# First attention: windowed softmax read from the own block of the full scores, shifts by block as extra contraction rows, a correction for the full softmax

## The chip, the cores and the metric

The kernel runs on one core of one Trainium2 chip. The metric is the device time of one execution in microseconds, the median of the runs shown. TensorE is called PE, VectorE DVE, ScalarE ACT, GpSimd POOL, and SyncE, which only issues DMAs here, SP.

## What is computed

Four layers on x of shape 8 x 512 x 128, float32: a first attention, a routed SwiGLU layer, a causal attention, a second expert layer. Only the first attention is touched. It has 16 heads of 8 columns and adds three softmaxes over the same q, k and v, cut here to what matters:

```python
qkv = x @ w_qkv                       # x is layer-normalised; 8 sequences of 512 tokens
s_loc = einsum("bnihd,bnjhd->bnhij", qw, kw) * scale   # 4 windows of 128 tokens
s_dil = einsum("bighd,bjghd->bghij", qd, kd) * scale   # tokens of equal index mod 4
s_glb = einsum("bihd,bjhd->bhij", q, k) * scale        # all 512 tokens
o = (softmax(s_loc) @ vw + softmax(s_dil) @ vd + softmax(s_glb) @ v) / 3
x = x + o @ w_out
```

## The kernel before, in words

`attention` is written once and called twice; `causal` is False for the first attention. Each sequence is a batch b of 8, and its 16 heads are four groups g of 4 heads. A slot n = 4b + g is one group of one sequence; there are 32. Queries and keys are split into three bfloat16 parts each, so one contraction over 72 of 96 partitions gives float32-like scores: `QS` and `KS`, one 512-column row per head, with the partitions above holding small extra rows.

Per slot the stages are these, each a function of the same name on every engine that takes part in it:

- `smax`: 16 matmuls (4 heads x 4 query blocks) of queries against all 512 keys into one of two PSUM banks `SM`; DVE reduces each to 16 maxima per query (4 windows x 4 phases) in `M`. PE may be two ahead of DVE.
- `maxima` (DVE): from `M` the row maxima of the three softmaxes, split in three bfloat16 parts (`maxima_parts`, `MT`); `rows`: PE transposes them, DVE copies them to `MR`, SP sends them to `QS` and `ML` by six DMAs.
- `scores`: twelve units into two halves of `ST`. Units 0 to 3 are mixed: one head's windowed scores in one bank and its dilated ones in the other, each by a matmul of 3 rows that subtracts the maxima (L422) and four of 128 columns (L430). Units 4 to 11 are full: two matmuls of 512 columns (L434), the shift among the contraction rows. ACT takes the exponential of each unit, 1024 columns, into a ring `E` of eight.
- `pv`: three rounds into `OA`, four heads side by side on 32 output columns each. Round 0 does the windowed and the dilated values (L457, 16 matmuls each), rounds 1 and 2 the full ones (L463). The matmuls are float32, so each counts as two in the trace.
- `evac` (ACT) copies `OA` out; `sel` (PE L472) turns it by query and picks outputs and sums; DVE divides and adds the three softmaxes (L679 to L690).

Projections (`proj`, `part1`, `left1`, `part2`, `left2`, `parts_out`, `stacks`), `values`, `heads_T` and `out_proj` come once a batch and are spread over its four slots.

The order is written out by hand in `slot(n)`: `put(i, name, which)` places an event behind unit i of slot n, and every engine walks the same list and takes the events it has a part in. Slot n carries the row maxima of slot n + 1 (the late ones, up to unit `CUT` - 1) and of n + 2 (the early ones). `maxima` of n + 1 stands behind unit `CUT` - 1, `rows` behind `CUT` + 1. Each engine runs its own list strictly in order. `MI` is one PSUM bank that `rows`, `sel`, `values` and the batch events take turns in.

## Time and profile before

| | |
|---|---|
| median of 3 runs | 2044.01 us |
| lowest and highest | 2037.59 and 2047.19 us |
| the profiled execution | 2029.46 us |
| its span | 2027.8 us |
| its mean granted TensorE clock | 0.898 |
| PE, DVE, ACT, POOL busy | 80%, 57%, 44%, 30% of the span |

The first attention fills 74 to 824 us of the span; ahead of it lie loads, the first projection and the first stacks. Rows of the trace name an instruction by its line, its engine and output <- input, with the tiles' names; the first attention's begin with w, the second's with c. A duration of a matmul holds its drain, so the time from one start to the next is what one costs in a row of them. An idle time stands with what ended it. The granted clock is 1 at 2.4 GHz and 0.5 at 1.2 GHz.

### The profile page before, as it was taken

The page shows a single profiled execution, that of the slowest core. Times are in us where ns is not written, and L with a number is a line of the kernel's source. Part 1 is how long each engine was busy: PE and PEld are TensorE (multiplying, and loading weights), DVE is VectorE, ACT ScalarE, POOL GpSimd, SP SyncE. Part 2 cuts the span into 40 slices and gives each one's busy share as a digit, 9 for nine tenths or more (in the row PEclk, how much of TensorE's full clock was granted, in tenths as well). Part 3 has the DMA queues.
Part 4 walks back from the last instruction along what each step waited for, and adds up shares of the span by engine and source line. Part 5 has one row for each costly group of instructions (what it writes and reads, how often), then busy time and mean ns, then how long its engine had stood idle before and what let it go on. Part 6 is the DMA issues. An engine that isn't in the chain of part 4 may idle for free. (4 is left out here: it accounts for less than half of the span.)

```text
span 2027.8 us, 35597 instructions
## 1 busy us (share of the span) xinstructions
PE 1630.1 (80%) x11387; PEld 888.1 (44%) x11489; DVE 1157.7 (57%) x3354; ACT 883.5 (44%) x1406; POOL 616.0 (30%) x879
## 2 busy tenths in 40 slices
PE   1899999999999999579899994468888888616683
PEld 1244444444444443355566663124444444514563
DVE  4756676656667664226333333468888877344584
ACT  1255555656565655431133331045555555402242
POOL 1001010101010100003522223376666533454467
PEclk8699999999999999679999997589999999557897
DMA  3110101111111100322011111233333220235442
GB/s 104 37 52 23 45 22 46 28 42 35 42 39 29 42 26 3 125 42 43 9 40 43 43 43 27 61 69 75 75 75 74 68 64 27 82 121 148 128 115 58
DMA packets 92786, 115.08 MB, mean 57 GB/s; under 512 B 13977, under 2 KB 76223, under 8 KB 92350
## 3 DMA queue, kind: packets, MB, share of 16 engines
q1 hardware_dynamic: 75710, 91.10, 16.5%
q0 software_dynamic: 16896, 21.69, 4.6%
q8 instruction: 99, 1.62, 0.3%
q14 instruction: 81, 0.66, 0.1%
HBM read 73.93 MB, written 39.34 MB: 56 GB/s over the span
## 5 line engine op out<-in xcount | busy, mean ns | idle before, releaser
L543 ACT ACTIVATE we<-wst 128x1024 f32<-128x1024 f32 x384 | 386.1, 1025 | 303.4 <-PE wst L430 158.8
L625 DVE TENSOR_REDUCE wm<-wsm 128x16 f32<-128x512 f32 x512 | 335.7, 685 | 259.5 <-PE wsm L393 255.6
L622 DVE CUSTOM_DVE_ANT_0 cjunk<-csm,const 128x128 bf16<-128x128 f32 (+3 forms) x512 | 232.5, 486 | 78.9 <-PE csm L393 70.3
L543 ACT ACTIVATE ce<-cst 128x896 f32<-128x896 f32 (+1 forms) x256 | 179.2, 704 | 186.0 <-PE cst L417 184.6
L393 PE MATMUL wsm<-wks,wqs 96*128 96x512 bf16 x512 | 191.3, 398 | 32.8 <-DMA wks<-qk_parts 20.2
L393 PE MATMUL csm<-cks,cqs 96*128 96x128 bf16 (+3 forms) x512 | 157.8, 315 | 69.1 <-DVE cnm L622 43.1
L772 POOL TENSOR_SCALAR_AFFINE_SELECT ce<-ce 128x256 f32<-128x256 f32 x256 | 125.3, 506 | 160.0 <-ACT ce L543 159.2
L434 PE MATMUL wst<-wqs,wks 128*128 128x512 bf16 x442 | 139.2, 385 | 9.5 <-issue 5.3
L1606 DVE TENSOR_TENSOR abhh<-absg,abup 128x512 f32<-128x512 f32 x72 | 49.5, 688 | 152.5 <-ACT absg L1585 152.5
L463 PE MATMUL woa<-we,wv 128*32 128x512 f32 x1024 | 132.0, 636 | 1.6 <-ACT we L543 1.6
L393 PEld LDWEIGHTS csm<-cks,cqs 96*128 96x128 bf16 x512 | 51.1, 100 | 182.6 <-DVE cnm L622 117.3
L1622 POOL DMA_INDIRECT abxb<-rows,asource x72 | 68.2, 947 | 162.3 <-DVE abys L1613 145.6
L417 PE MATMUL cst<-cqs,cks 128*128 128x384 bf16 (+3 forms) x480 | 106.6, 299 | 5.0 <-ACT ce L543 1.3
L422 PE MATMUL wst<-wml,const_b 3*128 3x512 bf16 x256 | 100.1, 391 | 9.3 <-ACT we L543 9.3
L430 PE MATMUL wst<-wqs,wks 96*128 96x128 bf16 x1024 | 105.9, 227 | 0.0
L1585 ACT ACTIVATE absg<-abup 128x512 f32<-128x512 f32 x72 | 43.0, 597 | 140.4 <-PE abup L1554 140.4
L393 PEld LDWEIGHTS wsm<-wks,wqs 96*128 96x128 bf16 x512 | 47.6, 98 | 122.5 <-DVE wm L625 61.0
L463 PE MATMUL coa<-ce,cv 128*32 128x512 f32 (+3 forms) x1024 | 92.3, 482 | 8.5 <-POOL ce L772 8.5
L430 PEld LDWEIGHTS wst<-wqs,wks 96*128 96x128 bf16 x1024 | 63.0, 108 | 60.1 <-issue 60.1
L761 POOL COPY wv<-wvs 128x128 f32<-128x128 f32 x32 | 9.3, 290 | 228.4 <-ACT wvs L503 200.2
L1554 PE MATMUL abup<-awg,abxt 128*128 x144 | 75.1, 604 | 2.3 <-ACT abxt L1591 2.3
L1574 PE MATMUL aby<-awd,abht 128*128 x576 | 76.2, 276 | 0.1
(318 smaller groups left out, 2987.7 us busy)
## 6 DMA issues: line engine op xcount, KB each, us to landing
wqs<-qk_parts SPq DMA_DIRECT2D x96, 96.0 KB
wks<-qk_parts SPq DMA_DIRECT2D x96, 96.0 KB
cqs<-qk_parts SPq DMA_DIRECT2D x96, 96.0 KB
cks<-qk_parts SPq DMA_DIRECT2D x96, 96.0 KB
b1r<-rows SPq DMA_DIRECT2D x40, 194.0 KB, 2.6
qk_parts<-wpt SPq DMA_DIRECT2D x48, 128.0 KB, 2.4
qk_parts<-cpt SPq DMA_DIRECT2D x48, 128.0 KB, 2.4
b0r<-rows SPq DMA_DIRECT2D x40, 130.0 KB, 2.5
```

The costliest lines, as they stand in the source:

```text
L393: pe.matmul(SM[:, j % 2, 0:keys], QS[0:MR0, h, t * P:(t + 1) * P], KS[0:MR0, h, 0:keys], start=True, stop=True, skip_group_check=True).the ...
L417: m = pe.matmul(st[:, at:at + width], KS[:, h, kb * P:(kb + 1) * P], QS[:, h, kb * P:S], start=True, stop=True, skip_group_check=True)
L422: pe.matmul(st[:, at:at + S], const["ones_b"][0:SPLIT, :], ML[:, g % 2, kind * HG + hs, :], start=True, stop=False, skip_group_check=True)
L430: m = pe.matmul(out, k, q, start=False, stop=(t == NT - 1), skip_group_check=True)
L434: m = pe.matmul(st[:, c * S:(c + 1) * S], KS[:, h, kb * P:(kb + 1) * P], QS[:, h, :], start=True, stop=True)
L463: m = pe.matmul(OA[VW * hs:VW * (hs + 1), S - width:S], V[:, kb, g * HG + hs, 0:VW], E[:, e_slot(g, HG * r + hs), at:at + width], start=(c ...
L543: act.activation(E[:, e_slot(g, i), 0:width], ST[:, (U * g + i) % 2, 0:width], ACT.Exp, scale=SCALE).then_inc(s_ex, 1)
L622: dve.tensor_tensor_reduce(JUNK[:, j % 4, 0:keys], SM[:, j % 2, 0:keys], const["mask_wide"][:, S - keys:S], 1.0, -3e38, ALU.add, ALU.max, ...
L625: dve.tensor_reduce(M[:, hs, t, :].rearrange("p (w f) -> p w f", f=DIL), SM[:, j % 2, :].rearrange("p (w i f) -> p w f i", w=NT, f=DIL), A ...
L772: pool.affine_select(e, e, [[0, 2], [1, P]], ALU.is_ge, 0.0, base=0, channel_multiplier=-1).then_inc(s_tri, 1)
L1554: m = pe.matmul(UP[:, i % 2, w, 0:F], XT[:, i % 2, :], weight[:, bass.ds(e * F, F)], start=True, stop=True)
L1574: m = pe.matmul(Y[:, j % 2, 0:D], HT[:, j % 2, c * P:(c + 1) * P], WD[:, bass.ds(e * HB * D + c * D, D)], start=(c == 0), stop=(c == HB - 1))
```

## The change

For the first attention only:

- The windowed softmax gets no scores of its own. Its scores are the own block of the full scores. Each block of keys kb has its own shift per query: the local maximum where kb is the query's own window, the maximum over the row elsewhere. So `QS` gets twelve rows of shifts (4 blocks x 3 bfloat16 parts) and three for the dilated shift; `KS` gets one-hot rows (`marks`) that pick the block's.
- There are ten units a slot: 0 to 7 are full (L437), 8 and 9 are dilated, two heads each (a shift matmul of 15 rows on partitions 96 to 110, L442, and four of 128 columns, L445).
- `pv` rounds 0 and 1 take each block's own quarter to the windowed columns of `V` and the rest to the full ones (ten pieces in place of four, L469); round 2 is the dilated one (L476).
- The full softmax's sum and output lack the own block in its scale, so a factor `E1`, the exponential of the difference of both maxima, joins them in `sel`.
- DVE's `maxima` has four more operations, one for each block's shifts (L688), and a difference (L692), and its parts are 80 columns wide instead of 48. ACT computes `E1` and copies `MR` (L585). POOL adds the three softmaxes. SP sends one DMA of rows per slot in place of six, and in the causal attention one in place of three.
- `CUT` is 3 instead of 4, and events move in `slot(n)`: `sel` from behind unit 4 to behind unit 5, the batch events likewise.

```diff
     L = "c" if causal else "w"
     KINDS = 1 if causal else 3
-    U = 8 if causal else 12
-    R = U // HG
+    SHIFTS = 1 if causal else NT + 1
+    U = 8 if causal else 10
+    R = 2 if causal else 3
     SMU = HG * NT
-    MROWS = KINDS * HG * SPLIT
-    CUT = 2 if causal else 4
+    MROWS = SHIFTS * HG * SPLIT
+    MR1 = MR0 + SHIFTS * SPLIT
+    CUT = 2 if causal else 3
     AHEAD = SMU * (U - CUT) // U
...
                 put(3, "evac", n - 1)
-                put(4, "sel", n - 1)
                 put(9, "pv", n, 1)
                 put(CUT - 1, "maxima", n + 1)
                 put(CUT + 1, "rows", n + 1)
+                put(5, "sel", n - 1)
...
-                elif i < HG:
-                    for kind in range(2):
-                        at = kind * S
-                        pe.matmul(st[:, at:at + S], const["ones_b"][0:SPLIT, :], ML[:, g % 2, kind * HG + hs, :],
-                                  start=True, stop=False, skip_group_check=True)
-                        for t in range(NT):
-                            q, k, out = QS[0:MR0, h, :], KS[0:MR0, h, :], st[:, at:at + S]
-                            if kind == 0:
-                                q, k, out = window(q, t), k[:, t * P:(t + 1) * P], window(out, t)
-                            else:
-                                q, k, out = q[:, t * P:(t + 1) * P], k[:, t::DIL], out[:, t * P:(t + 1) * P]
-                            m = pe.matmul(out, k, q, start=False, stop=(t == NT - 1), skip_group_check=True)
+                elif i < 2 * HG:
+                    for c in range(2):
+                        kb = 2 * (i // HG) + c
+                        m = pe.matmul(st[:, c * S:(c + 1) * S], KS[:, h, kb * P:(kb + 1) * P], QS[:, h, :],
+                                      start=True, stop=True)
                 else:
                     for c in range(2):
-                        kb = 2 * (i // HG - 1) + c
-                        m = pe.matmul(st[:, c * S:(c + 1) * S], KS[:, h, kb * P:(kb + 1) * P], QS[:, h, :],
-                                      start=True, stop=True)
+                        h, at = g * HG + 2 * (i - 2 * HG) + c, c * S
+                        pe.matmul(st[:, at:at + S], const["dil_b"][MR0:MR1, :], QS[MR0:MR1, h, :], start=True, stop=False,
+                                  skip_group_check=True)
+                        for t in range(NT):
+                            m = pe.matmul(st[:, at + t * P:at + (t + 1) * P], KS[0:MR0, h, t::DIL],
+                                          QS[0:MR0, h, t * P:(t + 1) * P], start=False, stop=(t == NT - 1),
+                                          skip_group_check=True)
                 m.then_inc(s_st, 1)
...
-                pe.wait_ge(s_tri if causal else s_ex, U * n + HG * (r + 1))
+                pe.wait_ge(s_tri if causal else s_ex, U * n + min(HG * (r + 1), U))
...
+                elif r < 2:
+                    for c in range(2):
+                        kb = 2 * r + c
+                        pieces = [(kb, kb + 1, 2 * VC)] + [(a, z, 0) for a, z in ((0, kb), (kb + 1, NT)) if a < z]
+                        for a, z, col in pieces:
+                            for hs in range(HG):
+                                e = E[:, e_slot(g, HG * r + hs), c * S:(c + 1) * S]
+                                m = pe.matmul(span(OA[VW * hs:VW * (hs + 1), :], a, z),
+                                              V[:, kb, g * HG + hs, col:col + VW], span(e, a, z),
+                                              start=(kb == 0 and a == 0), stop=False, skip_group_check=True)
+                else:
+                    for t in range(NT):
+                        for hs in range(HG):
+                            at = (hs % 2) * S + t * P
+                            m = pe.matmul(OA[VW * hs:VW * (hs + 1), t * P:(t + 1) * P], VP[:, t, g * HG + hs, :],
+                                          E[:, e_slot(g, 2 * HG + hs // 2), at:at + P], start=False, stop=(t == NT - 1),
+                                          skip_group_check=True)
                 m.then_inc(s_pv, 1)
...
+            def maxima(n, g, b, turn):
+                if causal:
+                    return
+                act.wait_ge(s_dif, n + 1)
+                if n >= NG:
+                    act.wait_ge(s_no, NNO * (n - NG + 1))
+                act.activation(E1[:, g, :], DIF[:, g, :], ACT.Exp, scale=SCALE).then_inc(s_e1, 1)
+
+            def rows(n, g, b, turn):
+                if causal:
+                    return
+                act.wait_ge(s_full, turn + 1)
+                if n:
+                    act.wait_ge(s_ml, 16 * n)
+                act.activation(MR[:, :], MI[0:MROWS, 0:S // 2].bitcast(BF16), ACT.Copy).then_inc(s_mr, 1)
...
-                dve.tensor_reduce(NM[:, 2 * HG:3 * HG, :], own, AX.X, ALU.max, negate=True).then_inc(s_mp, 1)
-                dve.wait_ge(s_mp, 4 * n + 3)
-                dve.tensor_reduce(NM[:, HG:2 * HG, :].rearrange("p h t -> p (h t)"),
+                dve.tensor_reduce(NM[:, NT * HG:(NT + 1) * HG, :], own, AX.X, ALU.max, negate=True).then_inc(s_mp, 1)
+                dve.wait_ge(s_mp, 8 * n + 3)
+                dve.tensor_reduce(LOC[:, :, :].rearrange("p h t -> p (h t)"),
                                   MD[:, :, :, :].rearrange("p h t k -> p (h t) k"), AX.X, ALU.max, negate=True
                                   ).then_inc(s_mp, 1)
-                dve.wait_ge(s_mp, 4 * n + 4)
+                dve.wait_ge(s_mp, 8 * n + 4)
+                for w_ in range(NT):
+                    dve.scalar_tensor_tensor(NM[:, w_ * HG:(w_ + 1) * HG, :], LOC[:, :, :], const["own"][:, w_:w_ + 1],
+                                             GLB[:, :, :], ALU.min, ALU.max).then_inc(s_mp, 1)
+                if n >= NG:
+                    dve.wait_ge(s_e1, n - NG + 1)
+                dve.tensor_tensor(DIF[:, g, :].rearrange("p (h t) -> p h t", h=HG), GLB[:, :, :], LOC[:, :, :], ALU.subtract
+                                  ).then_inc(s_dif, 1)
+                dve.wait_ge(s_mp, 8 * n + 8)
                 maxima_parts(n)
...
+                e1 = E1[:, g, :].rearrange("p (h t) -> p t h", h=HG)
+                dve.wait_ge(s_e1, n + 1)
+                dve.tensor_tensor(T1[:, :, :], e1, got[:, :, 0:HG, DH], ALU.mult).then_inc(s_no, 1)
+                dve.reciprocal(RL[:, :, 0:2 * HG, :], got[:, :, 0:2 * HG, DH:OC]).then_inc(s_no, 1)
                 dve.wait_ge(s_no, NNO * n + 1)
-                if b:
-                    dve.wait_ge(s_ot, b)
-                out = ON[:, :, g * HG * DH:(g + 1) * HG * DH]
-                to = out.rearrange("p t (h c) -> p t h c", h=HG) if causal else PR[:, :, :, :]
-                dve.tensor_tensor(to, got[:, :, :, 0:DH], RL[:, :, :, :].broadcast_to([P, NT, k, DH]), ALU.mult
+                dve.tensor_tensor(DEN[:, :, :], T1[:, :, :], got[:, :, 2 * HG:3 * HG, DH], ALU.add).then_inc(s_no, 1)
+                dve.wait_ge(s_no, NNO * n + 3)
+                dve.reciprocal(RL[:, :, 2 * HG:3 * HG, 0], DEN[:, :, :]).then_inc(s_no, 1)
+                dve.wait_ge(s_no, NNO * n + 4)
+                dve.tensor_tensor(T1[:, :, :], e1, RL[:, :, 2 * HG:3 * HG, 0], ALU.mult).then_inc(s_no, 1)
+                dve.wait_ge(s_no, NNO * n + 5)
+                dve.tensor_tensor(RL[:, :, 0:HG, 0], RL[:, :, 0:HG, 0], T1[:, :, :], ALU.add).then_inc(s_no, 1)
+                dve.wait_ge(s_no, NNO * n + 6)
+                if n:
+                    dve.wait_ge(s_on, 2 * n)
+                dve.tensor_tensor(PR[:, :, :, :], got[:, :, :, 0:DH], RL[:, :, :, :].broadcast_to([P, NT, k, DH]), ALU.mult
                                   ).then_inc(s_no, 1)
-                if causal:
-                    return
-                dve.wait_ge(s_no, NNO * n + 2)
-                dve.tensor_reduce(out, PR[:, :, :, :].rearrange("p t (k h) c -> p t (h c) k", k=KINDS), AX.X,
-                                  ALU.add).then_inc(s_no, 1)
...
-                dve.memset(KS[64:P, :, :], -1.0 if causal else 1.0).then_inc(s_ones, 1)
+                dve.memset(KS[64:P if causal else MR0, :, :], -1.0 if causal else 0.0).then_inc(s_ones, 1)
...
+            def sel(n, g, b, turn):
+                if causal:
+                    return
+                pool.wait_ge(s_no, NNO * (n + 1))
+                if b:
+                    pool.wait_ge(s_ot, b)
+                out = ON[:, :, g * HG * DH:(g + 1) * HG * DH].rearrange("p t (h c) -> p t h c", h=HG)
+                pool.tensor_tensor(out, PR[:, :, 0:HG, :], PR[:, :, HG:2 * HG, :], ALU.add).then_inc(s_on, 1)
+                pool.wait_ge(s_on, 2 * n + 1)
+                pool.tensor_tensor(out, out, PR[:, :, 2 * HG:3 * HG, :], ALU.add).then_inc(s_on, 1)
...
-                if n >= 2:
-                    sp.wait_ge(s_st, U * (n - 1))
-                for i in range(SPLIT):
-                    k = KINDS * HG * i
-                    sp.dma_start(QS[MR0 + i:MR0 + i + 1, g * HG:(g + 1) * HG, :],
-                                 MR[k:k + HG, :]).then_inc(s_ml, 16)
-                    if not causal:
-                        sp.dma_start(ML[i:i + 1, g % 2, :, :],
-                                     MR[k + HG:k + 3 * HG, :]).then_inc(s_ml, 16)
+                if n >= NG:
+                    sp.wait_ge(s_st, U * (n - NG + 1))
+                sp.dma_start(QS[MR0:MR1, g * HG:(g + 1) * HG, :], MR[:, :]).then_inc(s_ml, 16)
...
+    marks = np.zeros((P, NT), np.float32)
+    dil = np.zeros(P, np.float32)
+    for i in range(SPLIT):
+        at = MR0 + i * (NT + 1)
+        marks[at:at + NT] = np.eye(NT)
+        dil[at + NT] = 1.0
```

Two places show how the order moved. The first is PE's list from the last two row maxima of slot n + 1 (the `wsm` x2 that end them) to `rows`. L393 and L408 are row maxima, L434 and L437 full scores, L472 `sel`, L457 windowed and dilated PV, L400 and L415 `rows`. Before, behind the last two row maxima:

```order
L434 MATMUL wst<-wqs,wks 128x512 [waits wex]
L434 MATMUL wst<-wqs,wks 128x512
L393 MATMUL wsm<-wks,wqs 128x512 [waits wmx,wrd1]
L472 MATMUL wmi<-const,wos 128x108 [waits wev,wvs]
L472 MATMUL wmi<-const,wos 128x108 x3
L434 MATMUL wst<-wqs,wks 128x512 [waits wex]
L434 MATMUL wst<-wqs,wks 128x512
L393 MATMUL wsm<-wks,wqs 128x512 [waits wmx]
L457 MATMUL woa<-we,wv 32x4x32 [waits wev,wvc,wex]
L457 MATMUL woa<-we,wv 32x4x32 x15
L457 MATMUL woa<-we,wvp 32x128 x16
L400 MATMUL wmi<-const_b,wmt 36x128 [waits wms,wno]
```

And in the changed kernel, with those last two as the first row of row maxima:

```order
L408 MATMUL wsm<-wks,wqs 128x512 [waits wmx] x2
L437 MATMUL wst<-wqs,wks 128x512 [waits wex]
L437 MATMUL wst<-wqs,wks 128x512
L408 MATMUL wsm<-wks,wqs 128x512 [waits wmx,wrd2]
L408 MATMUL wsm<-wks,wqs 128x512 [waits wmx]
L437 MATMUL wst<-wqs,wks 128x512 [waits wex]
L437 MATMUL wst<-wqs,wks 128x512
L408 MATMUL wsm<-wks,wqs 128x512 [waits wmx]
L415 MATMUL wmi<-const_b,wmt 60x128 [waits wms,wno]
L415 MATMUL wmi<-const_b,wmt 60x128 x3
L437 MATMUL wst<-wqs,wks 128x512 [waits wex]
L437 MATMUL wst<-wqs,wks 128x512
```

Before, the second row maximum of the next set is followed by 32 PV matmuls, and `sel` stands ahead of it. Now two come together behind one unit and a third behind the next, and two more row maxima, a PV round and `sel` follow the rows shown.

The second place is DVE's list behind the same point, from the first operation of `maxima` on. Before:

```order
L636 TENSOR_REDUCE wnm<-wm 128x16 [waits wms,wmx]
L639 TENSOR_TENSOR wmd<-wm,const 128x256
L645 TENSOR_REDUCE wnm<-wm 128x16
L647 TENSOR_REDUCE wnm<-wmd 128x16 [waits wmp]
L661 CAST wmt<-wnm 128x12x4 [waits wmr,wmp]
L665 TENSOR_TENSOR wnr<-wnm,wmt 128x48 [waits wms]
L661 CAST wmt<-wnr 128x12x4 [waits wms]
L665 TENSOR_TENSOR wmt<-wnr,wmt 128x12x4 [waits wms]
L625 TENSOR_REDUCE wm<-wsm 128x16 [waits wsm]
L679 RECIPROCAL wrl<-wmi 128x48 [waits wfull]
L685 TENSOR_TENSOR wpr<-wmi,wrl 128x384 [waits wot,wno]
L690 TENSOR_REDUCE won<-wpr 128x4x32 [waits wno]
```

And in the changed kernel:

```order
L672 TENSOR_REDUCE wglb<-wm 128x16 [waits wms,wmx]
L675 TENSOR_TENSOR wmd<-wm,const 128x256
L681 TENSOR_REDUCE wnm<-wm 128x16
L683 TENSOR_REDUCE wloc<-wmd 128x16 [waits wmp]
L688 SCALAR_TENSOR_TENSOR wnm<-wloc,const,wglb 128x16 [waits wmp]
L688 SCALAR_TENSOR_TENSOR wnm<-wloc,const,wglb 128x16 x3
L692 TENSOR_TENSOR wdif<-wglb,wloc 128x16 [waits we1]
L705 CAST wmt<-wnm 128x20x4 [waits wmr,wmp]
L709 TENSOR_TENSOR wnr<-wnm,wmt 128x80 [waits wms]
L705 CAST wmt<-wnr 128x20x4 [waits wms]
L709 TENSOR_TENSOR wmt<-wnr,wmt 128x20x4 [waits wms]
L661 TENSOR_REDUCE wm<-wsm 128x16 [waits wsm] x5
```

The group of maxima has grown from 8 operations to 13, and `sel`, which stood one row maximum behind it, is now five behind and, as the diff shows, has seven operations instead of three.

## Rows read from the trace of the kernel before

**Rows 1.** The page: the span.

```profile
span 2027.8 us, 35597 instructions
```

**Rows 2.** Stretch of the first attention: stretch, length, busy and count per engine, clock, DMA.

```profile
core 0: us, PE busy (x) PEld busy (x) DVE busy (x) ACT busy (x) POOL busy (x), PEclk, DMA share, GB/s
74.00:824.00 750.00, 699.43 (x5889) 320.81 (x5958) 463.93 (x951) 433.27 (x484) 56.35 (x102) 0.97 0.12 33
```

**Rows 3.** Groups by line, 74 to 824 us: busy, mean ns, idle before, what ended it.

```profile
L543 ACT ACTIVATE we<-wst 128x1024 f32<-128x1024 f32 x383 | 385.2, 1025 | 303.4 <-PE wst L430 158.8 <-PE wst L434 142.4
L625 DVE TENSOR_REDUCE wm<-wsm 128x16 f32<-128x512 f32 x488 | 320.2, 685 | 245.0 <-PE wsm L393 242.2
...
L383 PE MATMUL wmi<-w,wxnT 128*128 128x128 f32 x112 | 23.1, 349 | 0.0
...
L369 PE MATMUL wmi<-wxnT,w 128*128 128x512 f32 x28 | 14.8, 612 | 1.3 <-ACT wxnT L503 1.3
```

**Rows 4.** Timeline of PE in one slot: start us, us, instruction, count, idle before.

```profile
438.25 0.39 PE L422 MATMUL wst<-wml,const_b 3*128 3x512 bf16 x1
438.57 0.40 PE L430 MATMUL wst<-wqs,wks 96*128 96x128 bf16 x4
...
439.47 0.59 PE L393 MATMUL wsm<-wks,wqs 96*128 96x512 bf16 x2
...
441.33 1.11 PE L472 MATMUL wmi<-const,wos 128*128 128x108 f32 x8 [0.22 <-ACT wos L550]
442.28 0.59 PE L434 MATMUL wst<-wqs,wks 128*128 128x512 bf16 x2
442.71 0.38 PE L393 MATMUL wsm<-wks,wqs 96*128 96x512 bf16 x1
443.02 1.08 PE L457 MATMUL woa<-we,wv 128*32 128x128 f32 x32
443.92 1.06 PE L457 MATMUL woa<-we,wvp 128*32 128x128 f32 x32
...
449.68 1.93 PE L463 MATMUL woa<-we,wv 128*32 128x512 f32 x16
```

**Rows 5.** Timeline of PE: the first and the thirty-first `sel`.

```profile
109.25 1.11 PE L472 MATMUL wmi<-const,wos 128*128 128x108 f32 x8 [0.23 <-ACT wos L550]
...
812.08 2.01 PE L472 MATMUL wmi<-const,wos 128*128 128x108 f32 x8 [1.26 <-ACT wos L550]
```

**Rows 6.** Timeline of DVE in the same slot: maxima and `sel` groups.

```profile
441.21 0.42 DVE L636 TENSOR_REDUCE wnm<-wm 128x16 f32<-128x256 f32 x1
...
443.69 0.69 DVE L625 TENSOR_REDUCE wm<-wsm 128x16 f32<-128x512 f32 x1
444.29 0.45 DVE L679 RECIPROCAL wrl<-wmi 128x48 f32<-128x48 f32 x1
...
445.88 0.68 DVE L625 TENSOR_REDUCE wm<-wsm 128x16 f32<-128x512 f32 x1
```

**Rows 7.** Groups by line, whole span: small DVE operations of both attentions.

```profile
L679 DVE RECIPROCAL wrl<-wmi 128x48 f32<-128x48 f32 x32 | 14.4, 450 | 31.1 <-PE wmi L472 31.1
...
L679 DVE RECIPROCAL crl<-cmi 128x16 f32<-128x16 f32 x32 | 8.2, 256 | 15.3 <-PE cmi L472 14.5
...
L665 DVE TENSOR_TENSOR cnr<-cnm,cmt 128x16 f32<-128x16 f32 x32 | 6.2, 195 | 1.1
```

**Rows 8.** Timeline of DVE at the start: the fills of QS and KS.

```profile
24.85 3.47 DVE L699 MEMSET wqs<- 64x4096 uint32 x1 [0.91 <-issue]
...
29.98 6.88 DVE L700 MEMSET wks<- 64x8192 bf16 x1 [1.66 <-issue]
```

**Rows 9.** Clock: two stretches, then a PV round and four matmuls of the second layer.

```profile
826.00:950.00 124.00, 91.74 (x385) 59.41 (x380) 51.43 (x191) 42.08 (x94) 19.54 (x33) 0.75 0.39 86
406.00:414.00 8.00, 8.00 (x50) 3.14 (x50) 1.98 (x3) 2.64 (x3) 0.00 (x0) 0.79 0.42 114
...
408.37 3.54 PE L463 MATMUL woa<-we,wv 128*32 128x512 f32 x16
...
844.42 1.09 PE L1390 MATMUL atp<-const,arows 128*128 128x128 f32 x4 [5.21 <-ACT arows L1442]
...
857.60 0.66 PE L1390 MATMUL atp<-const,arows 128*128 128x128 f32 x4 [2.22 <-ACT arows L1442]
```

More of the change, by code:

```diff
@@ L865, in setup @@
     C = sb("const", [P, c_dram.shape[1]])
[L866 removed]
+    CB = sb("const_b", [P, 4 * P], BF16)
     W0 = sb("w0", [P, 3 * D])
@@ L873, in setup @@
     const["mask_wide"] = C[:, at["open"][0]:at["mask_q"][1]]
-    for i, name in enumerate(("ident", "ones", "before")):
+    for i, name in enumerate(("ident", "ones", "before", "dil")):
         const[name + "_b"] = CB[:, i * P:(i + 1) * P]
```

119 lines of the change are left out of this document (68 added, 51 removed).

## The prediction

> **What bounds the kernel now.** I read the page for the span [rows 1], then the stretches for the first attention, which runs from about 74 to 824 us [rows 2]: PE is busy 699.4 of 750 us there, VectorE (DVE) 463.9, ScalarE (ACT) 433.3. So the question is what sets PE's pace. The groups by line say how the others stand [rows 3]: ACT's exponentials take 1025 ns each and ACT idles for 303 us in front of them, waiting for PE; DVE's row maxima (the wm reduces) take 685 ns and DVE idles 245 us, again for PE. The reader should see that neither is a bound as long as PE always has something that it may issue. The `sel` matmuls come once a slot: the 1st and the 31st start at 109.25 and 812.08 us [rows 5], so a slot lasts 702.83/30 = 23.4 us, and 32 slots make the stage.
>
> The timeline of one slot [rows 4] gives PE's issue prices, start to start, since a duration contains about 0.16 us of drain. A unit of mixed scores (438.25 to 439.47) costs 1.22. A full unit (442.28 to 442.71) costs 0.43, say 0.44. A row-maximum matmul costs 0.59 for two less the drain, 0.22. `sel` (441.33 to 442.28) costs 0.95. The windowed local PV (443.02 to 443.92) costs 0.90, the dilated one as much, and a round of full PV 1.93 less a little drain, 1.86. DVE's rows [rows 6] give the two groups that hold up its queue: maxima and their parts run from 441.21 to 443.69, 2.48 us; reciprocal, product and sum of `sel` from 444.29 to 445.88, 1.59 us. PE hides the first under `sel` and 1.8 us of windowed PV, both placed right after it. That is the fact that the change touches.
>
> **The change, part by part.** PE, a slot: four mixed units become two dilated ones, 2 x 1.22 = 2.44 off. The windowed local PV goes, 0.90 off. The ten pieces of own and foreign blocks stream the same columns as the four full ones, and the windowed row shows that a 128-column piece costs a quarter of a 512-column one (0.90/4 = 0.22 against 1.86/4 = 0.47 per block for two rounds, that is 0.93 per 512 columns), so they add nothing. In all 3.34 us a slot, 107 us in 32 slots, if PE never waited longer.
>
> ACT: two exponentials less (2.05 us), the copy of rows (some 0.6) and a tiny exponential more. It idles anyway: nothing, as long as it isn't held. The tiny exponential does hold it: it waits for DVE's difference, and behind it stand the exponential of unit 3, `evac` and the copy of rows. The difference is there some 1.9 us into DVE's group, and 1.9 + 0.25 + 1.02 = 3.2 is less than the wait of PE below. Nothing added.
>
> DVE: the maxima group gains four small operations, a difference, and parts of 80 instead of 48 columns. The nearest rows [rows 7] are 195 ns for a dependent 128x16 operation; independent ones overlap, so I take 0.09 to 0.15 for each of these five (0.6) and 0.17 for the longer parts: 2.48 + 0.77 = 3.25 us. Bounds: 2.48 (all hidden in each other's drain) and 3.9 (all five at full price and more on the parts). `sel` loses the final sum (to POOL) and 16 reciprocals but gets four dependent small operations and a reciprocal of 16 columns (256 ns against 450 ns for 48): 1.59 - 0.51 - 0.1 + 4 x 0.2 + 0.26 = 2.05 us. Bounds 1.6 and 2.4. The copy of rows (0.35) leaves DVE.
>
> Now the order, which the two places in the section on the change show. DVE does maxima after unit 2, then five row maxima, then `sel`. PE behind the 16th row-maximum matmul has two scores units and two such matmuls it may issue (there are two SM banks), then a third that needs DVE to be through the whole group. I count from the start of the 16th: 0.85 until DVE is done with the 15th, 0.65 for the 16th, 3.25 for the group, 0.65 for the next reduce, 0.19 back: **5.6 us**, in which PE has 0.22 + 2 x 0.44 + 2 x 0.22 = 1.5 us of work. It waits 4.1 us. `sel` and windowed PV, which covered this group before, now come later. Then PE works 4.3 us (row maximum, rows, a unit, two row maxima, PV, `sel`), and DVE's `sel` group holds the next row maxima: 0.2 + 2.05 + 0.65 + 0.19 = 3.1 us, with 1.3 of work in it. The rest of the loop is PE's: two dilated units, a full PV, three full units, the dilated PV, seven row maxima, 8.6 us with 0.35 of waiting. Sum 5.6 + 4.3 + 3.1 + 8.6 = 21.6 us, and the projections, values and so on, once a batch, 37.9/28 = 1.35 a slot from the two larger groups [rows 3]: **23.0 us**. The slot of now is 23.4, of which the clock (0.97 granted, [rows 2]) is 3%, 22 us over the stage, some of it at the start: 22.9 without. So the 107 us of PE's work turn into waits: +0.1 a slot, +3 us.
>
> Start: the fill of KS goes from 6.88 us to the form that took 3.47 [rows 8], ahead of the first stacks: -3 us. The four `marks` lie under the first stacks' transfers. POOL's two sums a slot and the one transfer of rows in place of six (three to one in the second attention) have 8 us before anyone needs them: nothing; if that cover went, it would be 1 us or less a slot.
>
> **The clock.** The rows show its price and its cause [rows 9]. In the stretch 406 to 414 the granted clock was 0.79, and the full PV in it took 3.54 us instead of 1.93: 1.6 us a drop. From 826 to 950, where PE was busy 91.7 of 124 us, in pieces, 0.75 was granted; after an idle time of 5.21 us four matmuls took 1.09 us (1.2 GHz), after one of 2.22 us the same four took 0.66 (2.4 GHz). A wait of 4.1 us lies between these. I take it that it costs one drop a slot, 0.8 of it on work: 1.3 x 32 = +42 us; half of the stage's present drops, which come in runs of mixed units, go: -7.
> The Trainium skill (TensorE: Matmul & The Clock Gate, "Why this matters for your kernels") asks for no long idle gaps of PE between bursts, or the clock falls to half rate. By that rule the new wait brings the drop in every slot, which is the forecast; the 5.21 us row agrees, and no row here shows a gap of just 4 us.
>
> Sum: +3 - 3 + 42 - 7 = **+35 us**. The profiled execution took 2029.5 us (span 2027.8), 14.6 below the median of 2044.0 and below the lowest of the three runs; I add the difference to the median: **2079 us**, own range 2058 to 2100.
>
> **Rivals.**
> A second drop a slot, at the 1.8 us wait for `sel`: another 42 us, 2120. For it: PE is then busy about 17 of 24 us, near the 74% of 826 to 950 us. Against: the 2.22 us row.
> No drop at all: 2044 + 3 - 3 = 2044. For it: the gap of 2.22 us cost none. Against: 4.1 lies nearer to the 5.21.
> DVE's groups at their lower bounds, 2.48 and 1.6: both waits shrink, 1.2 us a slot, 39 us; the long wait is then 3.3 us and the clock may hold: 2044 - 39 = 2005. This decides from a maxima group of some 2.6 us down. Against: the added operations depend on each other and can't all vanish.
> The shift matmul overlaps its neighbours. Its 15 rows lie on partitions 96 up, those of the four that follow on 0 to 95, while now both use the lowest ones. Then its 0.30 us (438.25 to 438.57 is the start of the next group, [rows 4]) is hidden, four times a slot: 38 us off, 2041 with the drops and 2003 without.
> The Trainium skill (TensorE: Matmul & The Clock Gate, "Part 3: Packing small matmuls") says that matmuls on different row groups run at the same time; by it this case would hold in full. Nothing in the trace runs on disjoint partitions, so no row bears it out; here both add into the same bank.
>
> **How the numbers follow.** Forecast 0.44, second drop 0.15, both slower; no drop 0.12; short DVE groups 0.15; overlap 0.14 (0.04 of it ends near no change). A measurement here can tell 0.5%, 10 us, from no change. Faster 0.25, same 0.16, slower 0.59. The range 2005 to 2125 leaves out the ends of the overlap and the worst of the drops.
>
> **What would show it.** PE's row maxima (wsm) waiting on DVE some 4 us once and 2 us once a slot; a maxima group of 3.25 us; PE's busy time in the stage down by about 100 us with the stage no shorter; many short stretches of granted clock 0.5, a mean of about 0.9. Wrong, if that wait is under 2 us, if the clock stays at 0.97, or if a dilated unit takes under 1.0 us.

## The result, and the profile after

| | median | lowest, highest | profiled span | its clock | first attention, 72 us to its last `heads_T` | clock there |
|---|---|---|---|---|---|---|
| before | 2040.8 us | 2036.4, 2047.2 | 2027.8 us | 0.898 | 760 us | 0.97 |
| changed | 2161.9 us | 2156.4, 2163.3 | 2154.7 us | 0.838 | 884 us | 0.81 |

The changed kernel is slower: the ratio is 1.0586 (1.0548 to 1.0623), 121 us by the medians. The sign was forecast, the size was not: 2162 us lies beyond the 2125 at the top of the range. The spans differ by 126.9 us and the first attention by 124; the rest took 1199 us after and 1196 before. So all but some 3 us of it is in the stage that the prediction looked at.

The page of the changed kernel, its span, busy times and clock, which answer to [rows 1]. What to see is the row PEclk: from its second digit on, where the first attention is, it stands at 6 to 8.

```profile
span 2154.7 us, 35568 instructions
...
PE 1654.8 (77%) x11361; PEld 908.6 (42%) x11361; DVE 1179.4 (55%) x3611; ACT 851.5 (40%) x1410; POOL 643.9 (30%) x943
...
PEclk8678788787878788876899999767999999757997
```

The stage as one stretch (columns as in [rows 2]), of the kernel before and then of the changed one:

```profile
72.00:832.00 760.00, 704.98 (x5918) 322.98 (x5988) 467.33 (x957) 435.67 (x486) 56.35 (x102) 0.97 0.12 33
```

```profile
72.00:956.00 884.00, 718.50 (x5855) 340.89 (x5853) 489.13 (x1205) 395.72 (x484) 84.50 (x166) 0.81 0.10 28
```

PE is busy longer with less work, because the same work takes twice the time at half the clock. With the busy time at the low clock (303 us, before 46) counted half it is 567 us, before 682: 115 less. Length times granted clock takes that out: it is what the stage would last at 2.4 GHz, and the rest is lost to the clock. Before, 760 x 0.97 = 737 and 23 lost; after, 884 x 0.81 = 716 and 168 lost. **The schedule got 21 us shorter and the clock took 145 us.** (Waiting at the low clock loses nothing and is counted here. It is little: I went through the stage in stretches of 1 us, and those below 0.75 are 324 us long with PE busy in 303 of them. The printed clocks have two digits. With the clock of every 1 us stretch added up, 25 us were lost before and 164 after: 15 us by the schedule and 139 by the clock. So the two terms are good to some 6 us.)

The waits of PE in the stage of the changed kernel (line, releaser, us in total, times, longest), then the group of the row maxima. Of before's matmul L393 the same view has 6.2 us in 28 times.

```profile
PE wsm L408 <- DVE wm L661: 140.8, 85, 4.1
PE wmi L362 <- DVE wpr L750: 7.3, 6, 1.2
PE wmi L415 <- DVE wmt L709: 3.7, 1, 3.7
```

```profile
L661 DVE TENSOR_REDUCE wm<-wsm 128x16 f32<-128x512 f32 x487 | 313.4, 684 | 258.0 <-PE wsm L408 256.3
```

The timeline of PE in one slot of the changed kernel, which answers to [rows 4]:

```profile
499.72 0.38 PE L408 MATMUL wsm<-wks,wqs 96*128 96x512 bf16 x1
...
501.49 0.60 PE L437 MATMUL wst<-wqs,wks 128*128 128x512 bf16 x2
505.41 0.39 PE L408 MATMUL wsm<-wks,wqs 96*128 96x512 bf16 x1 [3.33 <-DVE wm L661]
505.73 0.41 PE L415 MATMUL wmi<-const_b,wmt 128*60 128x128 bf16 x4
...
507.39 3.22 PE L469 MATMUL woa<-we,wv 128*32 128x128 f32 x40
510.54 1.14 PE L485 MATMUL wmi<-const,wos 128*128 128x108 f32 x8
...
512.60 0.38 PE L408 MATMUL wsm<-wks,wqs 96*128 96x512 bf16 x1
514.15 0.39 PE L408 MATMUL wsm<-wks,wqs 96*128 96x512 bf16 x1 [1.17 <-DVE wm L661]
514.47 0.38 PE L442 MATMUL wst<-wqs,const_b 15*128 15x512 bf16 x1
514.79 0.41 PE L445 MATMUL wst<-wqs,wks 96*128 96x128 bf16 x4
515.13 0.39 PE L442 MATMUL wst<-wqs,const_b 15*128 15x512 bf16 x1
```

And DVE's in the same slot, which answers to [rows 6]:

```profile
501.24 0.42 DVE L672 TENSOR_REDUCE wglb<-wm 128x16 f32<-128x256 f32 x1
...
502.66 0.67 DVE L688 SCALAR_TENSOR_TENSOR wnm<-wloc,const,wglb 128x16 f32<-128x16 f32 x4
503.24 0.17 DVE L692 TENSOR_TENSOR wdif<-wglb,wloc 128x16 f32<-128x16 f32 x1
...
504.46 0.52 DVE L709 TENSOR_TENSOR wmt<-wnr,wmt 128x80 bf16<-128x80 f32 x1
504.67 1.88 DVE L661 TENSOR_REDUCE wm<-wsm 128x16 f32<-128x512 f32 x3
...
511.72 0.18 DVE L737 TENSOR_TENSOR wt<-we,wmi 128x16 f32<-128x16 f32 x1 [3.36 <-PE wmi L485]
...
512.51 0.18 DVE L744 TENSOR_TENSOR wt<-we,wrl 128x16 f32<-128x16 f32 x1
512.73 0.17 DVE L746 TENSOR_TENSOR wrl<-wrl,wt 128x16 f32<-128x16 f32 x1
512.94 0.56 DVE L750 TENSOR_TENSOR wpr<-wmi,wrl 128x384 f32<-128x384 f32 x1
513.41 0.68 DVE L661 TENSOR_REDUCE wm<-wsm 128x16 f32<-128x512 f32 x1
```

The reader should see three things. The maxima group takes 504.67 - 501.24 = 3.43 us, and behind it the third row-maximum matmul starts 505.41 - 499.72 = 5.7 us after the 16th. The `sel` group takes 513.41 - 511.72 = 1.69 us and makes PE wait a second time. And the PV round behind the first wait took 3.22 us, where the same 40 matmuls take 1.94 at full clock.

Why the PV round took longer is seen in the stretches of this slot (columns as in [rows 2]):

```profile
486.00:497.00 11.00, 11.00 (x71) 4.82 (x71) 2.01 (x4) 2.89 (x4) 1.00 (x4) 0.53 0.12 40
501.00:507.00 6.00, 2.54 (x13) 0.87 (x12) 5.34 (x17) 3.35 (x6) 0.00 (x0) 0.97 0.00 0
507.00:510.00 3.00, 3.00 (x38) 1.63 (x40) 1.29 (x2) 0.74 (x1) 0.00 (x0) 0.50 0.09 26
510.00:517.00 7.00, 5.78 (x44) 2.93 (x36) 5.11 (x20) 2.96 (x3) 2.18 (x4) 0.99 0.00 0
517.00:524.00 7.00, 7.00 (x52) 2.95 (x53) 2.48 (x8) 1.54 (x2) 0.00 (x0) 0.52 0.27 67
```

In this slot the waits themselves lie at 2.4 GHz, and the clock falls to 1.2 GHz when PE is already at work again: once 1.6 us behind the end of the 3.3 us wait, and once 2.9 us behind the end of the 1.2 us wait. In the low stretches PE is busy throughout. In other slots the clock has already fallen when the long wait ends, as in this one, whose single row maximum takes 0.61 us instead of 0.39:

```profile
167.22 0.61 PE L408 MATMUL wsm<-wks,wqs 96*128 96x512 bf16 x1 [3.32 <-DVE wm L661]
```

In the stage after there are 56 low stretches and the start of one more, 324 us in all. That is 1.75 a slot of 5.8 us each, 3 to 11 us apiece. Of the 32 waits over 2.5 us, 22 have one beginning within 2 us of their end, mostly of 3 or 4 us; of the 29 waits of 1.2 us, 23 have one beginning 1 to 3 us behind them, mostly of 6 to 11 us. Some ten have no wait over 1 us near.

In the stage before I count 10, 48 us in all. The first, 15 us, is the stage's start, where the clock stands at 0.50 from 60 to 72 us already:

```profile
72.00:87.00 15.00, 14.59 (x54) 5.34 (x55) 9.64 (x26) 4.91 (x5) 1.80 (x4) 0.50 0.15 41
```

The other nine all begin at the end of a slot's mixed units or right behind it, eight of them with no wait of PE over 0.5 us in the 8 us ahead.

The prediction's sum lacked one thing beside the clock. Of those 32 waits over 2.5 us seven last 4.1 us. In just these seven slots the last operation of DVE's maxima group takes 1.3 us, and a POOL operation of the q and k preparation (L808) runs beside it; in the other 24 rows of that operation in the stage it takes 0.5 and POOL has nothing running. From the timelines of POOL and of DVE:

```profile
559.03 1.15 POOL L808 TENSOR_TENSOR wqr<-wqk,wpt 128x512 f32<-128x512 f32 x1 [3.44 <-ACT wpt L538]
```

```profile
559.24 1.32 DVE L709 TENSOR_TENSOR wmt<-wnr,wmt 128x80 bf16<-128x80 f32 x1
```

Why it takes longer there isn't shown; no run moves the POOL operation.

### The profile page after: what moved, and what is told of

It reads as the page before. It is cut to its first block and busy times, and to the rows that moved or that the text cites. A ratio compares the mean times of both kernels' runs of the same rounds, so it can differ in the third digit from the quotient of the medians.

```text
span 2154.7 us, 35568 instructions
## 1 busy us (share of the span) xinstructions
PE 1654.8 (77%) x11361; PEld 908.6 (42%) x11361; DVE 1179.4 (55%) x3611; ACT 851.5 (40%) x1410; POOL 643.9 (30%) x943
## 5 line engine op out<-in xcount | busy, mean ns | idle before, releaser
L556 ACT ACTIVATE we<-wst 128x1024 f32<-128x1024 f32 x320 | 322.6, 1021 | 343.1 <-PE wst L437 268.7
L408 PE MATMUL wsm<-wks,wqs 96*128 96x512 bf16 x512 | 212.5, 461 | 165.7 <-DVE wm L661 143.2
L408 PE MATMUL csm<-cks,cqs 96*128 96x128 bf16 (+3 forms) x512 | 160.7, 322 | 65.6 <-DVE cnm L658 39.7
L833 POOL TENSOR_TENSOR won<-wpr 128x128 f32<-128x128 f32 x32 | 14.5, 453 | 657.4 <-DVE wpr L750 657.4
L469 PE MATMUL woa<-we,wv 128*32 128x128 f32 (+2 forms) x2560 | 187.3, 461 | 0.0
L408 PEld LDWEIGHTS wsm<-wks,wqs 96*128 96x128 bf16 x512 | 55.2, 111 | 284.6 <-DVE wm L661 212.2
L437 PE MATMUL wst<-wqs,wks 128*128 128x512 bf16 x512 | 170.4, 419 | 1.1 <-ACT we L556 1.0
L469 PEld LDWEIGHTS woa<-we,wv 128*32 128x32 f32 x2560 | 97.3, 148 | 86.7 <-issue 80.2
L408 PEld LDWEIGHTS csm<-cks,cqs 96*128 96x128 bf16 x512 | 51.6, 101 | 181.0 <-DVE cnm L658 109.6
L432 PE MATMUL cst<-cqs,cks 128*128 128x512 bf16 (+3 forms) x512 | 115.6, 309 | 1.9 <-ACT ce L556 1.3
L1628 PE MATMUL abup<-awu,abxt 128*128 x144 | 74.4, 598 | 0.0
L437 PEld LDWEIGHTS wst<-wqs,wks 128*128 128x128 bf16 x512 | 44.8, 102 | 69.4 <-issue 43.4
```

What stands on the lines that cost most here:

```text
L408: pe.matmul(SM[:, j % 2, 0:keys], QS[0:MR0, h, t * P:(t + 1) * P], KS[0:MR0, h, 0:keys], start=True, stop=True, skip_group_check=True).the ...
L432: m = pe.matmul(st[:, at:at + width], KS[:, h, kb * P:(kb + 1) * P], QS[:, h, kb * P:S], start=True, stop=True, skip_group_check=True)
L437: m = pe.matmul(st[:, c * S:(c + 1) * S], KS[:, h, kb * P:(kb + 1) * P], QS[:, h, :], start=True, stop=True)
L469: m = pe.matmul(span(OA[VW * hs:VW * (hs + 1), :], a, z), V[:, kb, g * HG + hs, col:col + VW], span(e, a, z), start=(kb == 0 and a == 0), ...
L556: act.activation(E[:, e_slot(g, i), 0:width], ST[:, (U * g + i) % 2, 0:width], ACT.Exp, scale=SCALE).then_inc(s_ex, 1)
L1628: m = pe.matmul(UP[:, i % 2, w, 0:F], XT[:, i % 2, :], weight[:, bass.ds(e * F, F)], start=True, stop=True)
```

## The experiments

All ratios are to the kernel before, run on the same chip beside each (its medians were 2035.6 for the first four, 2044.3 for the next four, 2038.8 for the last two). "Lost" is length x (1 - clock) of the stage from 72 us to its end, the rest "at full clock". Gains and losses in us against the changed kernel are differences of medians taken beside other medians of the kernel before; by the ratios they come out up to 9 us otherwise (96 instead of 105 us for the cover). The main theory, A in the expectations, is that the waits cost little as time and much by the clock. Its rivals put the loss on the longer DVE groups as plain waiting (B), on new matmuls dearer than reckoned (C), on one long group as such (D), or on ACT being held (E). A1 and A2 ask whether the short wait or the short matmuls of the dilated units start the drops that remain.

### Fill the long wait with useless matmuls

```diff
+                if not causal and j == 2 and n >= 2 and FILL:
+                    pe.wait_ge(*emptied(turn))
+                    for _ in range(FILL):
+                        pe.matmul(MI[:, :], QS[0:MR0, h, t * P:(t + 1) * P], KS[0:MR0, h, :], start=True, stop=True, skip_group_check=True)
```

The changed kernel with `FILL` = 16, then 8. The results of these matmuls are never read.

> The changed kernel with 16 extra matmuls of 512 columns a slot, into the idle MI bank, ahead of the third early row maximum, where PE waits about 4 us for DVE. Their results are overwritten. They are 16 x 0.22 = 3.5 us of work that nobody needs. Theory A (the waits themselves cost nothing more than the 107 us saved; what made the kernel slower is that the granted clock falls in and after each wait, some 10 us of each slot's 28 at 1.2 GHz): with PE kept going the drop that follows this wait mostly goes, while the one at the wait for sel may stay; the mean clock in the stage rises from 0.82 to 0.88 or more and the kernel is 50 to 90 us faster than the changed one, 2070 to 2110 us. Theory B (the hand-over between PE and DVE sets the pace and the clock only mirrors it): no gain, 2160 us or some 5 us more. Theory C (the new matmuls, PV in ten pieces and shifts by 15 rows, are dearer than reckoned): no gain either, 2160 to 2270 us, as the extra work adds 3.5 us a slot where it is not hidden.

> The changed kernel with 8 extra matmuls in place of e1_fill16's 16, 1.7 us of work in the wait of some 4 us. Theory A (the loss is the granted clock): PE is kept going for part of the wait, so part of the gain comes, between the changed kernel's 2162 and the 2074 of the run with 16: about 2115 us, stage clock 0.86. Theory B (the fuller queue helped in some other way): the same 2074 us or the 2162 us of no filling, not in between.

Sixteen: 2073.8 us, 1.0163 (1.0122 to 1.0204). **The kernel does some 3.5 us more on PE in a slot and is 88 us faster.** The timeline of PE in a slot of it:

```profile
518.29 3.62 PE L409 MATMUL wmi<-wks,wqs 96*128 96x512 bf16 x16
522.59 0.39 PE L414 MATMUL wsm<-wks,wqs 96*128 96x512 bf16 x1 [0.68 <-DVE wm L667]
...
524.22 1.94 PE L475 MATMUL woa<-we,wv 128*32 128x128 f32 x40
...
529.70 0.39 PE L414 MATMUL wsm<-wks,wqs 96*128 96x512 bf16 x1 [1.17 <-DVE wm L667]
```

The filler stands where the wait was, and the PV round is back at 1.94 us. This is one of the seven slots with the wait of 4.1 us: from the last full unit before the filler to the row maximum behind it are 4.73 us, 4.74 in such a slot of the changed kernel, so the row maximum starts no later. The 1.17 us wait is as before: 18 of 30 such waits still have a low stretch close behind, and 24 low stretches of 138 us are left in the stage:

```profile
72.00:882.00 810.00, 741.47 (x6333) 364.33 (x6331) 487.91 (x1204) 394.10 (x484) 84.48 (x166) 0.92 0.11 31
```

Lost to the clock: 65 us instead of 168. At full clock the stage is 745 us, 29 more than in the changed kernel. This is as theory A has it; B and C had no gain.

Eight: 2138.1 us, 1.0467 (1.0403 to 1.0531), 24 us better than none. I had expected about 2115, half of what sixteen bring; it is a quarter. It lies between none and sixteen, where the rival named for this run had no place. The stage shows 862 us at 0.85, 129 lost. The clock does not answer in proportion to the wait.

### Bring the cover back

```diff
-            put(2 if causal else 1, "pv", n - 1, R - 1)
+            put(2 if causal else 3, "pv", n - 1, R - 1)
-                put(5, "sel", n - 1)
+                put(4, "sel", n - 1)
```

The changed kernel with the dilated PV behind unit 3 and `sel` behind unit 4, so that PE has them to do while DVE is in its maxima group.

> The changed kernel with two events moved: the dilated PV of the slot before from behind unit 1 to behind unit 3, and sel from behind unit 5 to behind unit 4. Nothing is added or left out. PE then has 0.9 us of PV in the wait for the maxima group, and DVE meets the work of sel before it has fallen behind. Theory A: both waits shrink by 0.9 us together and with them the drops: a slot of 25 instead of 28 us, 2060 to 2090 us. Theory B: the slot shortens by the 0.9 us of wait alone, 28 to 30 us over 32 slots, 2130 us. Theory C: 2130 to 2160 us.

2057.3 us, 1.0116 (1.008 to 1.0152): 105 us back, 3 us beyond what A expected at best, and far from B and C. PE's waits for `wm` fall from 140.8 to 63.5 us; 688 us at full clock, 103 lost.

### Cut the group as well

```diff
+                put(3, "max_b", n + 1)
+                put(4, "max_c", n + 1)
+                put(5, "max_e", n + 1)
+                put(5, "rows", n + 1)
-                put(CUT + 1, "rows", n + 1)
...
-                    put(9, "out_proj", b - 1)
...
+                    put(6, "out_proj", b - 1)
...
```

The edit above, and DVE's `maxima` cut in three behind units 2, 3 and 4, so that row maxima come in between; the small exponential and `rows` behind unit 5; `out_proj` a slot later. No operation is added or removed.

> As e2_cover, and the maxima group of DVE is cut in three: the three operations that read the row maxima behind unit 2, local maxima, shifts and difference behind unit 3, the three bfloat16 parts behind unit 4, with row-maximum reduces between them; rows go behind unit 5, the small exponential behind unit 5, and the output projection to the next slot. The same operations, in another order. PE then never waits over 1.5 us for a row maximum. Theory A: the clock stays at 0.95 or more in the stage and the 3.3 us of PE's work that the change removed come through: a slot of 20.5 to 21.5 us against 23.4 before, 1960 to 1990 us, faster than both kernels. Theory B: a slot of 23 us or so, about 2040. Theory C: 2100 us or more.

**1943.4 us, 0.9537 (0.9499 to 0.9575): 4.6% below the kernel before and 10% below the changed one.** It is also some 17 us below what I had expected at best. The stage, then PE's waits in it:

```profile
72.00:750.00 678.00, 612.11 (x5853) 308.42 (x5852) 481.29 (x1204) 393.75 (x484) 84.83 (x166) 0.95 0.13 37
```

```profile
PE wsm L411 <- DMA wks<-qk_parts: 21.3, 7, 4.6
PE wmi L418 <- DVE wpr L761: 20.0, 27, 1.0
PE wsm L411 <- DVE wm L664: 5.7, 19, 1.9
```

At full clock 644 us, 93 less than before: now most of the 107 us of PE's work that the change removes comes through (some 4 of the 93 are the earlier start). 34 us are lost to the clock. What is late next is the first stacks of a batch (21.3 us in 7 times). In a slot, DVE's group is cut like this (timeline of DVE):

```profile
403.15 0.42 DVE L675 TENSOR_REDUCE wglb<-wm 128x16 f32<-128x256 f32 x1
...
404.12 1.29 DVE L664 TENSOR_REDUCE wm<-wsm 128x16 f32<-128x512 f32 x2
405.32 0.41 DVE L690 TENSOR_REDUCE wloc<-wmd 128x16 f32<-128x256 f32 x1
...
406.44 0.69 DVE L664 TENSOR_REDUCE wm<-wsm 128x16 f32<-128x512 f32 x1
407.04 0.35 DVE L716 CAST wmt<-wnm 128x80 bf16<-128x80 f32 x1
```

### Cutting without cover, in the changed kernel and in the one before

The three pieces with `pv` and `sel` left where the change put them; and, in the kernel before, `maxima` cut in two:

```diff
-                put(CUT + 1, "rows", n + 1)
+                put(3, "max_b", n + 1)
+                put(4, "max_c", n + 1)
+                put(5, "max_e", n + 1)
...
+                put(5, "rows", n + 1)
...
```

```diff
+                put(CUT - 1, "maxima", n + 1)
+                put(4, "max_c", n + 1)
                 put(4, "sel", n - 1)
                 put(9, "pv", n, 1)
-                put(CUT - 1, "maxima", n + 1)
...
```

> The changed kernel with DVE's maxima group cut in three and rows and the small exponential behind unit 5, as in e3_split, but with the dilated PV and sel where the change has them. The long wait of 4 us splits in shorter ones, yet sel then stands right behind the last third. Theory A: about 26 us a slot against 28, 2090 to 2130 us, since PE's total wait in a slot stays near 6 us: the cut needs PV between its parts to be worth much. Theory D (cutting the group is what made e3_split fast, the other moves are incidental): under 2000 us.

> The kernel before with its maxima group cut in two: the three operations that read the row maxima behind unit 3, the fourth and the parts behind unit 4 ahead of sel, one row-maximum reduce between them. There the group was hidden under sel and windowed PV already. Theory A: within 10 us of before, 2025 to 2045 us; the cut pays only where the group is exposed. Theory D: some 60 us faster, as the cut by itself pays.

2105.0 us, 1.0291 (1.0222 to 1.036), and 2044.9 us, 1.0003 (0.9978 to 1.0028). The first gains 57 us, the second nothing. In the changed kernel the wait was only divided and moved: PE waits 134 us for the two tiles `wm` and `wpr` in place of 148, and of the 47 us that the stage is shorter, 42 come from the clock (837 us at 0.85). The timeline of PE:

```profile
508.59 0.39 PE L411 MATMUL wsm<-wks,wqs 96*128 96x512 bf16 x1 [1.28 <-DVE wm L664]
...
513.78 0.41 PE L418 MATMUL wmi<-const_b,wmt 128*60 128x128 bf16 x4 [1.87 <-DVE wpr L761]
```

So a long group as such isn't the main cause. Cover gave 105 us, cutting 57, both together (with `out_proj` moved, which wasn't tried alone) 218, and only together do they leave no wait above 1 us in a usual slot. That this is why the two add up to more than their sum is argued, not shown.

### The reverse: the same wait in the kernel before

```diff
+                for _ in range(LOAD):
+                    dve.tensor_reduce(SPARE_[:, _, :], flat, AX.X, ALU.max, negate=True)
```

Eight useless reduces of 256 columns in DVE's maxima group of the kernel before, whose PE work stays untouched.

> The kernel before with eight extra reduces of 256 columns on DVE in each maxima group, written to a spare tile: the group grows from 2.48 by 8 x 0.34 = 2.7 us to some 5.2 us, which sel and the windowed PV no longer cover. PE's work is unchanged. Theory A: PE waits some 2.5 to 3 us more a slot, 85 us over the stage, and the clock falls in it: another 40 us or more, 2160 to 2200 us in all, with the clock in the stage at 0.90 or lower. Theory B: 2120 to 2130 us, the waits alone, whatever the clock. Theory C says nothing of it.

2151.6 us, 1.0563 (1.0534 to 1.0592), nearly as slow as the changed kernel. A had expected 2160 to 2200 us and 0.90 or less in the stage, B 2120 to 2130: the result lies between the two, nearer to A. Timelines of DVE and of PE in a slot:

```profile
502.03 2.70 DVE L645 TENSOR_REDUCE wspare<-wm 128x16 f32<-128x256 f32 x8
```

```profile
508.13 0.40 PE L402 MATMUL wmi<-const_b,wmt 128*36 128x128 bf16 x4 [3.01 <-DVE wpr L689]
```

The stage is 116 us longer, 876 us at 0.91: 797 at full clock, 60 more, and 79 lost, 56 more. The waits for DVE, here in front of `rows`, account for the first (87.8 us instead of 11.2, more than the 60), the drops for the second: 37 low stretches of 157 us in place of 10 of 48, mostly of 3 or 4 us. A wait of 3 us brings a loss of clock without any of the change's matmuls, but only some 55 us of the 145.

### The hold on ACT

```diff
+                put(4, "max_e", n + 1)
...
```

The small exponential moves from behind unit 2 to behind unit 4, out of the way of ACT's exponential of unit 3.

> The changed kernel with the small exponential on ACT taken from behind unit 2 to behind unit 4, so that ACT is no longer held by DVE's difference with the exponential of unit 3 and evac queued behind it. Nothing else. The prediction priced that hold at nothing, as PE waits longer for DVE anyway: 2160 us, within 10 us of the changed kernel. Theory E (ACT held by DVE is the wait that takes the time): 30 us or more faster.

2157.9 us, 1.0549 (1.0482 to 1.0615): 4 us, within the spread. The two waits of the slot are still 3.33 and 1.17 us. ACT held nobody up here.

### The second wait

```diff
-        NNO = 2 if causal else 7
+        NNO = 2
-                dve.tensor_tensor(T1[:, :, :], e1, got[:, :, 0:HG, DH], ALU.mult).then_inc(s_no, 1)
-                dve.reciprocal(RL[:, :, 0:2 * HG, :], got[:, :, 0:2 * HG, DH:OC]).then_inc(s_no, 1)
+                dve.reciprocal(RL[:, :, :, :], got[:, :, :, DH:OC]).then_inc(s_no, 1)
...
```

DVE's `sel` is one reciprocal and one product; once without and once with the sixteen fillers. These kernels leave out the own block's part in the full softmax's sum and factor.

> The changed kernel without the correction for the full softmax on DVE: five small operations of sel are left out and one reciprocal of 48 columns stands for the two, so the sel group falls from 1.7 to 1.05 us and PE's wait behind it from some 1.5 to 0.9 us. Left out: the own block's part in the full softmax's sum and factor. What is open is where the drops that don't follow the long wait come from. Theory A1 (the short wait for sel starts them): the drops over the dilated units mostly go, a slot falls from 28.1 to 26 us or less, 2090 us. Theory A2 (the short matmuls of the dilated units start or hold them by themselves, whatever the wait): only the 0.65 us of wait goes, 20 us in all, 2140 us, and the clock in the stage stays at 0.81 to 0.82.

> As e9_short_sel, with e1_fill16's 16 extra matmuls in the long wait. Both of PE's waits are then under 1 us. Theory A1: the clock in the stage is 0.95 or more and the kernel takes 2020 to 2040 us. Theory A2: the stretches at 1.2 GHz over the dilated units stay as in e1_fill16 (stage clock 0.92), 2055 us.

2097.8 us, 1.0286 (1.0242 to 1.033), and 2040.3 us, 0.9982 (0.9952 to 1.0013). Leaving out 20 us of DVE (469.1 us busy in the stage in place of 489.1), 0.63 a slot, shortened the stage by 57 us: 13 at full clock and 44 by the clock (124 lost in place of 168). The short wait has a large price of its own; A1 had expected 2090 us, A2 2140. With both waits dealt with, the stage is 768 us at 0.95, 38 lost in 20 low stretches: 130 of the 145 us that the clock had taken are back. The stage of both:

```profile
72.00:899.00 827.00, 681.41 (x5854) 328.98 (x5853) 469.06 (x1044) 395.94 (x484) 84.48 (x166) 0.85 0.10 30
```

```profile
72.00:840.00 768.00, 717.91 (x6334) 356.99 (x6333) 467.24 (x1044) 394.24 (x484) 84.74 (x166) 0.95 0.11 33
```

The four kernels with and without each wait share out the loss to the clock: both waits 168 us, the short alone 65, the long alone 124, neither 38. So the long wait has 86 to 103 us of it and the short one 27 to 44, although the longer low stretches stand behind the short one. A2 holds for part of the rest. Without both waits, 14 of the 20 low stretches begin over dilated units or within 2 us behind them, with no wait of PE over 0.6 us in the 6 us ahead; with the long wait alone, 17 of 50 do.

## Why the prediction was right or wrong

**What bounds the kernel.** Right: PE's pace, set by its waits on DVE, and ACT no bound. PE's busy time, forecast to fall by about 100 us, rose by 14, as half clock stretched it; with that taken out it fell by 115.

**PE's removed work, 3.34 us a slot.** Borne out. A dilated bank takes 514.47 to 515.13, 0.66 us, 1.32 for a unit instead of 1.22; PV pieces cost nothing extra (1.94 us for the 40 rows of a round, against 1.93 for the 16 of a full round in [rows 4]). With waits gone, 93 us of the 107 showed.

**DVE's groups.** 3.25 was forecast and 3.43 us measured; 2.05 and 1.69. The first was 4.25 in the seven slots with POOL beside it, which no term held. The second gives half of the next term's miss.

**The waits.** 5.6 us from the 16th to the third row maximum was forecast, 5.7 measured. Of the 4.1 us of waiting in it, 3.33 stand in one piece, the rest in short ones ahead. Behind `sel` a wait of 1.8 us was forecast, and 1.17 came.

**Work for waits: +3 us.** With the start's -3 that is 0; measured were -15 to -21 us at full clock, a slot of 22.4 us (716/32) where 23.0 was forecast. The start gives 4 (the first row maximum at 48.40 instead of 52.27 us). The `sel` group, 0.36 us shorter a slot than I had it, gives 32 x 0.36 = 12. So this term was off by some 15 to 20 us, and to the safe side: it is not what took the time out of the range, and by luck it hid part of what did.

**The clock: this step failed.** "I take it that it costs one drop a slot, 0.8 of it on work: 1.3 x 32 = +42 us; half of the stage's present drops ... go: -7". Both sizes in it were off. There were 1.75 drops a slot, not one, and one lasted 5.8 us and took half of that, 2.9, from work, not 1.3. 56 x 2.9 = 162, less the 24 of before (half of 48), is 138 of the 145 us that the two stretches give. The price of 1.6 us came from one drop in a stretch without waits [rows 9], and I carried it to slots whose waits follow each other, where the clock stays down over the dilated units and the PV behind them. By the runs with and without each wait, the long one had 86 to 103 us of it, where the sum had 42, and the short one 27 to 44, where it had none. In the kernel before the price was nearer: with a 3 us wait in each slot it lost 56 us more, 1.75 a slot against 1.3. The mechanism was right, as the filled wait (-88), the same wait put in the kernel before (+116) and the shortened `sel` (-64) show; -21 + 145 is the stage's own +124. The -7 for drops of mixed units that go was not tested by itself; 15 of the 48 us of low clock before were the stage's start, which it could not remove.

**The rivals.** The second drop at the wait for `sel` is what happened for most slots; 2120 was its price, with the same 1.3 us a drop. The argument against it, that a gap of 2.22 us in [rows 9] cost no clock, was a gap in another stage with another work around it; here 1.2 us did. With 0.15 for it, the prediction held it for one of the less likely courses. No drop at all fell: 0.81 granted. Short DVE groups fell: 3.43 us, though `sel` with 1.69 was near its bound of 1.6. The overlap of the shift matmul fell: the next group starts 0.32 us behind it, as before (438.25 to 438.57 is 0.32 too, not 0.30; and 2079 - 38 less the drops' 35 is 2006, not 2003).
The Trainium skill (TensorE: Matmul & The Clock Gate, "Part 3: Packing small matmuls") has matmuls on different row groups run at once. Here, on rows 96 up and 0 to 95, they did not, by those 0.32 us; both add into the same bank, so this is no test of the rule for different banks. The Trainium skill (TensorE: Matmul & The Clock Gate, "Why this matters for your kernels") asks for no long idle gaps. The trace agrees with the direction (waits of 3.3 us, 0.81 granted), and the shortened `sel` shows that waits of 1.2 us count as well: 44 us less lost to the clock without them.

**What stays open.** What brings the drops that are left (nine behind the start before, 15 low stretches of 72 us in the version cut and covered) isn't shown. They mostly begin in dilated or mixed units or right behind them, with no wait near: eight of the nine, and 14 of the 20 that remain without both waits. That says where, not why. These units are short matmuls, of 128 columns or a few rows, and no run here changes them with the waits left as they are.

## What to carry to other kernels

Before a change takes work off TensorE, look for what that work was hiding: here two VectorE groups, of 3.4 and 1.7 us in the changed kernel, stood without cover, and the work that was saved came back as waits. Price a new repeated wait twice, once as time and once by the granted clock of the work behind it, and count both from slots that have such waits; length times clock, stage by stage, separates the two. Then put back cover and cut the group that holds the queue, both together: the same operations in another order took 2162 us to 1943.

## What the runs showed of the hardware

- Useless matmuls in a wait made the kernel 88 us faster (2162 to 2074), and half as many only 24.
- A wait of 1.2 us in each slot cost more by the clock than by itself: the shortened `sel` gave back 13 us at full clock and 44 of clock.
- PE at half clock is often fully busy: 11.00 of 11.00 us at 0.53 from 486 to 497, over dilated units, row maxima and a PV round. A stage with PE 93% busy (705 of 760 us) still had nine low stretches behind its start, each at the end of the short matmuls of the mixed units.
- Small dependent operations of 128x16 on DVE cost about 0.22 us from start to start (512.73 - 512.51), and four independent ones 0.58 us together (502.66 to 503.24).
- The same DVE operation (L709, 128x80 float32 in, bfloat16 out) took 1.3 us in the seven slots in which a POOL operation ran beside it, and 0.5 us in the other 24.
